# A kernel of four chained attention layers on one core: the third attention moved one turn later, value tiles with zeros between heads, steps placed anew

## The reference, cut to what matters

```
s_new = k_l v_l^T + w_l * s ; out = r_l (faaaa * k_l v_l^T + s)       (layer 2, for each token)
attn = softmax(q k^T + mask) ; out = attn v                           (layers 0, 1 and 3)
```

## Time and profile before

| | |
|---|---|
| device time, median of 3 runs | 1263.58 us (1258.09 to 1264.42) |
| the profiled execution | 1264.44 us, its span 1262.5 us |
| PE busy | 1127.0 us (89%) |
| PEld busy | 765.1 us (61%) |
| DVE busy | 956.6 us (76%) |
| ACT busy | 651.5 us (52%) |
| POOL busy | 261.0 us (21%) |
| granted TensorE clock, mean | 0.945 |

### The profile page before, as it was taken

How to read it: one execution, slowest core, us unless ns; L and a number is a source line. 1 busy time by engine, 2 the same in 40 slices (tenths; PEclk the granted TensorE clock), 3 DMA queues, 4 the chain that set the end, 5 groups by cost and what they waited for, 6 DMA issues and landing times. The chain is left out here.

```text
span 1262.5 us, 24184 instructions
## 1 busy us (share of the span) xinstructions
PE 1127.0 (89%) x7776; PEld 765.1 (61%) x7776; DVE 956.6 (76%) x3401; ACT 651.5 (52%) x2483; POOL 261.0 (21%) x349
## 2 busy tenths in 40 slices
PE   5878899999999998999999998999999998897656
PEld 4564666665665666666666666666666666554434
DVE  2707697789967998789968998689968998675834
ACT  1528343784448553774448553674438553582024
POOL 3210223102410214102420214102321214101310
PEclk9788899999999999999999999999999999898858
DMA  8000000000000000000000000000000000000000
GB/s 296 2 9 20 1 2 1 22 2 15 2 21 2 16 1 1 22 2 16 1 22 2 12 5 1 22 2 15 1 22 2 6 11 1 1 2 11 1 1 9
DMA packets 18092, 18.91 MB, mean 15 GB/s; under 512 B 7216, under 2 KB 16432, under 8 KB 17712
## 3 DMA queue, kind: packets, MB, share of 16 engines
q1 hardware_dynamic: 17968, 17.37, 4.6%
HBM read 15.27 MB, written 2.10 MB: 14 GB/s over the span
## 5 line engine op out<-in xcount | busy, mean ns | idle before, releaser
L831 ACT ACTIVATE E<-S,nmax 128x128 f32<-128x128 f32 (+1 forms) x1024 | 424.1, 416 | 229.4 <-DVE nmax L1020 215.1
L1020 DVE CUSTOM_DVE_ANT_0 S<-psS,mb 128x128 f32<-128x128 f32 (+1 forms) x1024 | 264.3, 320 | 87.7 <-PE psS L534 64.4
L494 PE MATMUL ring<-slot,w_l 128*128 128x256 f32 x992 | 251.5, 400 | 14.0 <-DVE slot L1202 5.2
L494 PEld LDWEIGHTS ring<-slot,w_l 128*128 128x128 f32 x992 | 188.8, 198 | 60.0 <-issue 12.8
L548 PEld LDWEIGHTS psT<-ident,E 128*128 128x128 f32 x1280 | 146.2, 147 | 128.1 <-ACT E L831 73.3
L534 PE MATMUL psS<-keys,slot 32*128 32x512 f32 (+1 forms) x768 | 194.4, 581 | 30.1 <-DVE nmax L1020 19.0
L1035 DVE COPY ET<-psT 128x512 f32<-128x512 f32 x320 | 206.2, 681 | 7.8 <-PE psT L548 7.8
L548 PE MATMUL psT<-ident,E 128*128 128x128 f32 x1280 | 203.8, 293 | 7.8 <-DVE ET L1035 3.2
L831 ACT ACTIVATION_READ_ACCUMULATOR E<-S,nmax 128x1 f32 x1024 | 191.6, 187 | 0.0
L504 PE MATMUL ring<-w_l,slot 128*128 128x256 f32 (+1 forms) x640 | 151.9, 384 | 7.7 <-DVE slot L1051 5.8
L504 PEld LDWEIGHTS ring<-w_l,slot 128*128 128x128 f32 x640 | 115.3, 194 | 36.6 <-issue 10.7
(11 more groups left out here) (119 smaller groups left out, 1183.3 us busy)
## 6 DMA issues: line engine op xcount, KB each, us to landing
slot<-in_ctx SPq DMA_DIRECT2D x8, 256.0 KB, 2.7
slot<-in_x SPq DMA_DIRECT2D x8, 256.0 KB, 2.7
w_l<-in_wl SPq DMA_DIRECT2D x1, 2048.0 KB, 11.2
out<-slot SPq DMA_DIRECT2D x8, 256.0 KB, 2.1
w_l<-in_wl SPq DMA_DIRECT2D x2, 768.0 KB, 7.1
w_l<-in_wl SPq DMA_DIRECT2D x1, 1152.0 KB, 9.9
m0i<-in_m SPq DMA_DIRECT2D x8, 128.0 KB, 3.2
mb<-in_m SPq DMA_DIRECT2D x8, 128.0 KB, 2.8
```

What stands on the lines that cost most here:

```text
L494: m = pe.matmul(b[:, a, :], w[:, k, m0 + a * P:m0 + (a + 1) * P], src[:, k, :], start=(k == 0), stop=(k == kt - 1))
L831: ins = act.activation(E[:, g % RING_E, h * w:(h + 1) * w], S[:, g % RING_S, h * w:(h + 1) * w], ACT.Exp, bias=nmax[:, g % 4, h:h + 1], sc ...
L1020: ins = dve.tensor_tensor_reduce(S[:, g % RING_S, h * w:(h + 1) * w], psS[g % 2][:, h * w:(h + 1) * w], bias[:, bb, :], -1.0, HUGE, ALU.ad ...
```

## The change

1. **A fourth stream.** Attention 3 with `inv3`, `sum3`, `o3` (`FINAL`) leaves the back stream and runs one turn later: beside the front of the pair two after. `k3` and `v3` go from the front to the back stream. The phases are now `start`, `first`, `second`, five turns `steady`, `closing`, `last`, `end`. `OUT` and `X4` get tiles of their own (slots 23, 24).
2. **The order of the steps is new everywhere.** `HEAD` and `TAIL` interleave the steps of neighbouring phases. In a turn the jobs of attention 3 stand between the end of attention 0 and step `vr3`, and SP stores the output before it loads the next context.
3. **Value tiles with zeros between heads.** V0 and V3 hold 16 values, 16 zeros, 16 values and so on (V1: 8 and 24); a product picks 32 columns by `window`, with the head's values at the wanted place. One VectorE instruction fills a tensor instead of four.
4. GpSimd's copies of the weights v and g by lane (`weights_by_lane`) go from ahead of the first keys to step `x1T` of `first`; TensorE waits for them at `t` of `second`.

```diff
+def window(head, place, d):
+    at = 32 * head + 32 - d - d * place
+    return slice(at, at + 32)
...
-    *jobs(1, 11, 13), "x4T", *jobs(1, 13, 15), "q3", *jobs(1, 15, 16), *jobs(3, 0, 1), *jobs(1, 16, 18), "inv1",
...
+    *jobs(3, 0, 2), "inv0", *jobs(0, 16, 18), "r2", "mg",
+    *jobs(3, 2, 3), "v2", "sum0", *jobs(3, 3, 4), *jobs(0, 19, 20), "d2", "decay", *jobs(3, 4, 6), "vr0", "cols",
...
-HAS = {"start": (0,), "first": (0, 1), "steady": (0, 1, 2), "closing": (1, 2), "last": (2,)}
-TIMES = {"start": 1, "first": 1, "steady": TURNS - 2, "closing": 1, "last": 1}
+HAS = {"start": (0,), "first": (0, 1), "second": (0, 1, 2), "steady": (0, 1, 2, 3), "closing": (1, 2, 3), "last": (2, 3),
+       "end": (3,)}
+TIMES = {"start": 1, "first": 1, "second": 1, "steady": TURNS - 3, "closing": 1, "last": 1, "end": 1}
...
-IN_ORDER = {"start": [], "first": [0, 1], "steady": [0, 1, 3], "closing": [0, 1, 3], "last": [3]}
+IN_ORDER = {"start": [], "first": [0, 1], "second": [0, 1], "steady": [0, 3, 1], "closing": [0, 3, 1], "last": [3], "end": [3]}
...
-        rT, X3, OUT = cm(18), tm(18), tm(18)
+        rT, X3, OUT = cm(18), tm(18), tm(23)
-        vT, tmpv, X4 = cm(20), tm(20), tm(20)
+        vT, tmpv, X4 = cm(20), tm(20), tm(24)
...
-        V0 = sb("V0", [2, PAIR, 2, C])
-        V1 = sb("V1", [PAIR, 4, C])
-        V3 = sb("V3", [PAIR, 2, C])
+        V0 = sb("V0", [2, PAIR, 16 * 32 + 16])
+        V1 = sb("V1", [PAIR, 8 * 32 + 24])
+        V3 = sb("V3", [PAIR, 16 * 32 + 16])
...
-                                                  v[:, t * P + 32 * c:t * P + 32 * c + 32], e,
+                                                  v[:, window(8 * t + 4 * half + c, half, 16)], e,
...
                 def values16(name, dst):
                     dve.wait_ge(sems["product"], product(name))
-                    for half in range(2):
-                        for ct in range(CT):
...
+                    d = dst[:, :, 16:].rearrange("p b (h x) -> p b h x", x=32)[:, :, :, 0:16]
+                    v = bank(phase, i, name).rearrange("p b (h d) -> p b h d", d=16)
...
+                if final is not None:
+                    sp.wait_ge(leaves("o3"), left("o3"))
+                    sp.dma_start(out[final], OUT).then_inc(sems["out_done"], 16)
+                if entry is not None:
                     if phase != "start":
                         sp.wait_ge(leaves("aT"), left("aT"))
-                    sp.dma_start(CX, ctx_in[shift:][entry]).then_inc(sems["c_in"], 16)
+                    sp.dma_start(CX, ctx_in[entry]).then_inc(sems["c_in"], 16)
```

More of the change, by code:

```diff
@@ L451, in _ @@
             program("first", None)
-            for i in range(TURNS - 2):
+            program("second", None)
+            for i in range(TURNS - 3):
                 program("steady", i)
@@ L455, in _ @@
             program("last", None)
+            program("end", None)
             sp.wait_ge(sems["out_done"], TURNS * 16 + 1)
@@ L780, in program @@
                         token_major("o3", attnT, W3["o"])
-            program("start", None)
-            program("first", None)
-            pe.wait_ge(s_w2, 18 * 16)
-            pe.wait_ge(s_lanes, 2)
-            for i in range(TURNS - 2):
-                program("steady", i)
-            program("closing", None)
-            program("last", None)
+            for part in PARTS:
+                program(part)
         @block.scalar
@@ L834, in exps @@
                     ins.then_inc(sems["exps"], 1)
-                for step in steps_of(phase):
+                for phase, i, step in order_of(part):
+                    turn, before, product, left = counts(phase, i)
+                    first_job = FIRST[phase]
+                    earlier_left = counts(*phase_before(phase, i))[3] if phase != "start" else None
                     if step[0] == "job":
@@ L974, in _, with program @@
             dve.wait_ge(s_setup, 1)
-            def program(phase, i):
-                turn, before, product, left = counts(phase, i)
-                first_job = FIRST[phase]
+            def program(part):
                 def norm_stats(src, n):
```

392 lines of the change are left out of this document (205 added, 187 removed), and 3 rows, old and new, of the table TAIL.

## The result

The changed kernel takes 1274.0 us, the median of five runs (1270.1 to 1282.52); the kernel before, 1259.23 in five runs. The ratio is 1.0112, with a 95% interval of 1.0078 to 1.0145: **slower by 1.1%**. The prediction had 1251, faster. Its sum took 12.5 us off; measured are 14.8 us more. (The 1263.6 from which it reckoned was the median of three runs; with two more the kernel before stands at 1259.23.)

The account below looks back on a forecast made before the run. VectorE was taken to bound A, TensorE B, the norm chain C; parts 141 + 131 + 718.5 + 142.5 + 117 gave a 1250 us span, 12.5 less, so 1251 us from the median. Range 1233 to 1270.

Parts of the forecast that it names:

- full turn: One turn from `apply2` to `apply2`: 143.7 us against 143.4 before; five of them 718.5.
- C: Turn slice from the end of `o1` to the next `apply2`: 10.4 us, with a 0.9 us TensorE wait.
- A: Turn slice from `apply2` to the last gather, set by VectorE: 75.4 us, before 62.9.
- Second: The second part, a first full turn without attention 3: 131 us, with A at 63.5.
- the gain that the sum had at the ends: Parts outside the five full turns: head 144.8 to 141, second part 131 with no sixth full turn; whole span -12.5 us.
- B: Turn slice from the last gather to the end of `o1`, set by TensorE: 57.9 us, before 66.4.
- Pure pairs: Attention 1 job pairs with no product between take 3.30 us; five such pairs add 1.9 us to B.
- Shared port: Rival, chance 0.13: VectorE and GpSimd exclude each other between `apply2` and last scan; A grows 4.4, turn 148.1, total 1273.
- Closing: The closing part: 142.5 us against 140.5 before, with A 75.4, B 56.7 and C 10.4.
- First: Start and first part: 144.8 becomes 141 us (weight copies -2.2, `k3` and `v3` -3.6, less covered chain +2.5).
- The value tiles: One VectorE instruction per value tensor saves 1.2 us of VectorE, about 1.1 of it in the chain from `o1` to `xaT`.
- No gain at the ends because the clock falls: Rival, chance 0.05: second part nearly as long as a full turn, as TensorE's clock falls where it waits; total 1262 us.

Follow-up runs that it names:

- both holes filled: The changed kernel with three idle matmuls in each of the two holes at a turn's start: 1259.87 us.
- the first alone filled: The changed kernel with six idle matmuls only ahead of `xaT`, the hole ahead of `t` left open: 1271.5 us.
- `k0l` there: The changed kernel with product `k0l` moved from ahead of `sum1` to behind `o1` in the five full turns: 1270.37 us.
- the long fills: The changed kernel with idle matmuls in both holes of every turn start, the first part and the last part, before counts were halved: 1253.66 us.
- the holes filled: The changed kernel with six idle matmuls in each of the two holes at a turn's start: 1259.83 us.
- the filled kernels: Idle matmuls everywhere, counts halved: the changed kernel 1247.04 us; the kernel before, with new value tiles and late weights, 1224.38 us.
- two experiments: The kernel before with the new value tiles alone: 1259.4 us; the changed kernel with the old value tiles: 1277.87 us.

## Why the prediction was wrong, point by point

- **The step that failed** is the sum of the full turn at its start: "with a wait of 0.9 for TensorE at the turn's start" in C, and `shift1` "now stands ahead of the first masks and waits for `xaT` (+1.0...)" in A. Both price a wait at its own length and put the clock behind it at nothing. The first wait was seen (1.6 us). The second, 2.0 us ahead of `t`, the working did not have for TensorE at all: `shift1` was costed for VectorE alone, while TensorE has only the scores of two jobs to do meanwhile. In place of the 17 us at 1.2 GHz that five turns had before, there are 55; at 0.37 to 0.5 us for each of the 38 more that is 14 to 19 us, and the turns were 16.9 over the sum. With both holes filled they are 142.8, 0.9 under it. With the first alone filled 27 us at 1.2 GHz stay (48 with `k0l` there), so the wait that the working lacked is the weightier.
- **Not all of the miss is clock.** Second and closing were 8.8 and 10.9 over the sum, which the first part's -8.7 hides in part. With the long fills second is 137.0 at a clock of 1.00 and closing 147.3 at 0.99, still 6.0 and 4.8 over (some 1.7 of each is the fill). And with the clock kept up in both orders the changed one is not 12.5 us faster but 8 to 20 slower, 3 to 10 by estimate when the fills and what is left at 1.2 GHz are taken off. So the gain that the sum had at the ends is missing without any fall of the clock; why closing loses 7 us and more was not settled.
- The granted clock was read only where it was worst (0.73 in the last part). The full turn's 0.99 hid a fall in every turn, at the very place that the change thins out. Rows in slices of a few microseconds would have shown 0.90 over the first 17.
- **A, B and C** were right where the clock stands: 74.6, 57.4 and 10.8 with the holes half filled, for 75.4, 57.9 and 10.4. In the changed kernel A is 76.5 with 6.8 us at 1.2 GHz and 79.5 with 13.7. The 57.9 has a small slip (five pairs at 0.36 more are 1.8, not 1.9), which changes nothing. VectorE in A is busy 70.5, as summed. One more scan pair is long, and pairs `vr4` to `vr7` behind each other are all long:

```profile
586.28 0.99 DVE L1231 TENSOR_TENSOR slot<-slot,shifted 128x512 f32<-128x512 f32 x1
...
628.93 1.28 DVE L1269 TENSOR_TENSOR_SCAN SS<-wP,kv 128x258 f32<-128x258 f32 x2
...
630.83 1.95 DVE L1269 TENSOR_TENSOR_SCAN SS<-wP,kv 128x258 f32<-128x258 f32 x2
...
633.39 1.94 DVE L1269 TENSOR_TENSOR_SCAN SS<-wP,kv 128x258 f32<-128x258 f32 x2
```

  The first pair after other VectorE work (628.93) took 1.28, the next ones 1.95 and 1.94. The two products of `ruk` fell from 1.77 to 0.9 together, as said.
- **Pure pairs** of attention 1 cost what the first part had shown, 3.1 to 3.5 us:

```profile
677.28 1.13 PE L569 MATMUL psS<-keys,slot 32*128 32x512 f32 x4
...
680.73 1.13 PE L569 MATMUL psS<-keys,slot 32*128 32x512 f32 x4
...
683.80 1.13 PE L569 MATMUL psS<-keys,slot 32*128 32x512 f32 x4
```

- **Shared port** (0.13, the rival that was slower): not what made A long. A was 75.9 with the holes filled, far from the 79.2 from which it was to decide; the two turns that are past it (79.5) are those with 13.7 us at 1.2 GHz. The one mixing product that met keys for attention 3 (line 1231, 586.28 above) took 0.99 and not 0.69:

```profile
585.54 1.19 POOL L1394 TENSOR_TENSOR keys<-k3T,in 128x256 f32<-128x256 f32 x2 [4.42 <-PE psS L569]
```

  That is 0.3 us a turn for the 2.4 that the rule of the Trainium skill (SBUF — State Buffer, Who interferes with whom) would allow if all of them met. The trace agrees with the rule for keys as it does for Z, and with what the prediction took, that most keys meet something else: one meeting in five. The dearer meeting lies where the prediction did not look, ahead of A: `apply2` beside the keys for attention 0, 2.09 us for 0.8. It is in C of both kernels, and now TensorE waits for it.
- **Second** (131, measured 139.8): "A 63.5 (VectorE again)" was wrong. Its own list puts `aT`, `k3`, `v3` and `u3` ahead of the last gather, 6.3 us of TensorE, and there TensorE (67.1 us), not VectorE (57.3), is the busier one. A is 73.3 here and 70.5 with the long fills:

```profile
132.30:205.60 73.30, 67.10 (x432) 44.35 (x432) 57.25 (x141) 29.80 (x95) 18.40 (x23) 0.93 0.02 5
```

- **Closing** (142.5, measured 153.4): A 79.9 for 75.4, of which 2.8 went with the filling; B 64.0 for 56.7. B has 13.7 us at 1.2 GHz, worth 5 to 7, and its row is

```profile
1087.40:1151.40 64.00, 58.61 (x367) 38.57 (x367) 40.04 (x188) 36.64 (x150) 5.97 (x8) 0.89 0.02 6
```

  58.61 busy, as much as in the earlier trace rows, at a clock of 0.89. Even filled, closing keeps 148.8 (147.3 with the long fills): the moved jobs were subtracted from a part whose waits I hadn't read. Which wait takes the rest stays open.
- **First** (141, measured 132.3): right in its pieces, as the filled kernels show (127.7 against 128.7 before, both with the weights by lane late; for the rest the working had -3.6 + 2.5), but it wanders by itself: 131.3 to 141.1 us in the profiles of six kernels whose first part is the changed one's, with 14 to 44 us at 1.2 GHz. The profile of the kernel before had caught a long one, 144.8, and the sum starts from it. The 8.7 under the sum lie in this base and in the spread, and not in the working.
- **The value tiles** were priced at 1.1 in C and the first part. They are worth nothing that two experiments could see: `apply2` ends with GpSimd's keys, wherever the short instructions leave it.
- *No gain at the ends because the clock falls* stood among the rivals with 0.05, for the second part above all; it had the right mechanism but not the place where most of it fell, the full turns, and took it to take back a gain and not to add a loss.
- **Last and end** (117, measured 113.5): 3.5 under. How much of that is the clock (42 us at 1.2 GHz, 63 in the part before) was not tested by itself.

## What to carry to other kernels

Before a change takes work away from beside a dependent chain, slice the profile finely where the chain is bare and read TensorE's granted clock there: a hole can be paid twice, once in its length and once in 0.37 to 0.5 of the time that the engine then spends at 1.2 GHz. Identical turns that differ in length are the sign of it. Look, too, at whether the last step of the bare chain stands beside work of an engine that lengthens it, as `apply2` beside the keys. In a kernel of one core whose chains leave holes of one to five microseconds, idle matmuls slightly shorter than the holes are worth trying first, with their length read from a profile and not reckoned: 2.9% here, with the order of before, together with new value tiles and late weights, which alone brought nothing clear. Most of it came at the two ends; the fills at the turns' starts alone brought 0.5%.
